# Third graph layer: elementwise work in a new order over four groups, and its own rows turned into columns by transposing transfers of SyncE

## The chip, the cores and the metric

The kernel runs on one core of one Trainium2 chip. A core has a matrix engine (TensorE, PE), a vector engine (VectorE, DVE), a scalar engine (ScalarE, ACT), a general engine (GpSimd, POOL), a queueing engine (SyncE, SP), and 16 DMA engines that move data between HBM and on-chip memory (SBUF) and inside SBUF. The matrix engine writes into PSUM, here eight banks of 128 partitions x 512 fp32. Each engine runs its own instruction stream in order, and streams meet only at semaphores. The metric is the device time of one execution in microseconds (us).

## What is computed

Four graph layers on 4096 nodes with 128 features each, every one as `x = x + layer(relu(layernorm(x)))`, over one 4096 x 4096 adjacency matrix of zeros and ones: an attention layer, a mean-aggregation layer, a gated layer (GRU), and a hyperbolic layer. The change touches the third:

```python
h = relu(layernorm(x))
agg = adj @ h
msg = relu(agg @ W_msg.T + b_msg)
gi = msg @ W_ih.T + b_ih
gh = h @ W_hh.T + b_hh                       # the layer's own rows
r = sigmoid(i_r + h_r)
z = sigmoid(i_z + h_z)
n = tanh(i_n + r * h_n)
x = x + (1 - z) * n + z * h
```

and the first half of the fourth, which the kernel computes group by group beside it:

```python
h = relu(layernorm(x))
e = exp_map_zero(log_map_zero(h) @ embed)    # norms, artanh, tanh per row
e = h_add(e, embed_bias)                     # a point in the ball
t = log_map_zero(e)                          # its tangent: operand of adj @ t
p1 = h @ layer[:128]                         # stored, used later
```

`adj @ t` and everything behind it is the fourth layer's second half and is not changed.

## The kernel before

**Tiling.** The 4096 rows are 32 tiles of 128 rows, and 8 groups of 4 tiles (`NT`, `TG`, `NG`). Most 128 x 512 operations handle one group. The adjacency matrix stays in SBUF as fp8. An operand row is held as two fp16 parts, a high and a low one, so a product with the adjacency matrix takes 64 matmuls of 128 x 512 for a group of output columns (32 tiles times 2 parts): one *step*. Steps are numbered through: 8 to 15 (`s`) are the third layer's aggregations, 16 to 23 the fourth's; 16 to 19 are called FIRST to FOURTH. A step's matmuls are `k` = 0 to 63 (L1432).

**TensorE's order** is written by hand. The tables `after`, `late`, `back` and `own` (L1381 to L1386) say at which `k` of a step a small piece of another group is put in. Take group `g`, whose aggregation is step `g+8`. During the step after it, TensorE does `hidden_gates` (k = 1: nine matmuls of L1286, own rows as columns `hT16` times three weight matrices, into banks 4, 5, 7), `message` (k = 6), `message_gates` (k = 11, L1329 to L1331) and `update_back` (k = 44: transposes of L1336, which bring the new state back into rows). One step later follow `new_transposes` (k = 15), `embed` (k = 26) and `own_part` (k = 32; L1279). `own_transposes` (k = 62 of the group's own step, L1272) turns the group's rows, kept in `hs_b` (a part of `region_op`), into columns in bank 2; ScalarE copies them into `hT16` (L1061).

**ScalarE and VectorE** each run one function `layer2` per iteration, for three groups at once: group `g` (gates, update), group `g-1` (new rows, their norms, embedding) and group `g-2` (ball point, tangent). Iterations 2 to 7 are a hardware loop. Semaphore names say what is ready: `u_ready` the updated state, `row16_ready` the new rows in two parts, `z_ready` the ball point, `coef_ready` the factor of its tangent, `hs_ready` an operand group, `rz_ready` the two sigmoid gates, `t_ready` the argument of the tanh of `n`. VectorE sums `hT16`'s two parts at L790. GpSimd takes the square roots: `norm_h`, `norm_e`, `norm_z`, and `inverse_deviation`.

**SyncE** in this stretch only stores `p1_sb`, the group's own product with `layer[:128]`, into `p1_rows` in HBM (L311), one group after another; ScalarE fills the single buffer `p1_sb` at L1141 after waiting for the store of the group before (`p1_out`), and takes a tanh (L1083) right behind it.

**The end of the layer.** Behind step 15 TensorE has FIRST to FOURTH as filling, cut into pieces (L1497 to L1516): FIRST, SECOND and THIRD can run up to k = 56 and FOURTH to k = 24 before they need `hs_ready` of the last group, the end of its chain.

Of the kernel before, what the change touches and what calls it, by code (L numbers as in the profile page):

```python
# [17 lines left out]
D = 128  # L18
NT = N // P
TG = 4  # L20
# [35 lines left out]
BANKS_3 = (0, 1, 6, 7)  # L56
UNITS = ((0, 1), (2, 3), (4, 5), (6,), (7,))
# [16 lines left out]
def build_graph_stack(nc, x_rows, adj_pieces, proj, consts0, matrices, vectors, p1_rows, out_rows):  # L74
# [8 lines left out]
    with ExitStack() as ctx:  # L83
# [96 lines left out]
        def pair(i, part):  # L180
# [4 lines left out]
        STEPS_2 = 59  # L185
# [44 lines left out]
            "pre_tr", "pre_hT", "agg_full", "aThi_ready", "aT_ready", "l1_self", "l1_neigh",  # L230
# [49 lines left out]
        def _(sp):  # L280
# [59 lines left out]
        def _(dve):  # L340
# [421 lines left out]
            def layer2(a, b, c):  # L762
                A, B, E = a is not None, b is not None, c is not None
                if A:
                    low_aggregate(a, NG)
                if B:

                    dve.wait_ge(S["rs_ready"], b + 2 * NG + 1)
                    normalised(b, lambda t: tile(dT, t)).then_inc(S["xnew_ready"], 1)
                if E:  # L770
                    ball_rows(lambda t: tile(bank[3], t), b3e)
                if B:
                    dve.wait_ge(S["row16hi_ready"], b + 1)
                    v.scalar_tensor_tensor(row16[:, 1, :, :], tiles(dT), 0.0, row16[:, 0, :, :], ALU.max,
                                           ALU.subtract).then_inc(S["row16_ready"], 1)

                part = BOTH if B and E else H_ONLY if B else Z_ONLY
                count = b + 1 if B else NG + 1
                if E:
                    dve.wait_ge(S["nrmz_ready"], c + 1)  # L780
                if B:
                    dve.wait_ge(S["nrmh_ready"], b + 1)
                if B or E:
                    artanh_start(part)
                if B:
                    me.step(copy(ssh[:, group_of(b)], C(SSH)))
                if B or E:
                    artanh_series(part, count)
                if A:
                    me.step(v.tensor_tensor(dT, hT16[:, 0, :], hT16[:, 1, :], ALU.add))  # L790

                    dve.wait_ge(S["gates_full"], a + 1)
                    dve.wait_ge(S["rz_ready"], a + 1)
                    me.link(v.scalar_tensor_tensor(rT, bank[7], b_hn, rT, ALU.add, ALU.mult))
                    v.scalar_tensor_tensor(rT, rT, w_unsplit[:, M_HN:M_HN + 1], bank[6], ALU.mult,
                                           ALU.add).then_inc(S["t_ready"], 1)

                    dve.wait_ge(S["n_ready"], a + 1)
                    me.link(v.scalar_tensor_tensor(dT, dT, 1.0 / SPLIT, rT, ALU.mult, ALU.subtract))
                    me.link(v.tensor_tensor(zT, zT, dT, ALU.mult))  # L800
                    v.tensor_tensor(zT, zT, rT, ALU.add).then_inc(S["u_ready"], 1)
                if B or E:
                    artanh_finish(part, count)
                if E:
                    v.tensor_scalar(C(COEF), pair(KAP, Z_ONLY), SPLIT, None, ALU.mult).then_inc(S["coef_ready"], 1)
                if B:
                    dve.wait_ge(S["sqe_ready"], b + 1)
                    dots(lambda t: tile(bank[3], t), b3e, w_unsplit[:, M_EMB:M_EMB + 1])
                    dve.wait_ge(S["nrme_ready"], b + 1)
                    exp_argument(pair(KAP, H_ONLY))  # L810
                if A:
                    dve.wait_ge(S["uT_full"], a + 1)
                    v.tensor_tensor(x[:, group_of(a), :], x[:, group_of(a), :], tiles(bank[7]), ALU.add).then_inc(S["x3_ready"], 1)
                    dve.wait_ge(S["x3_ready"], a + 1)
                    statistics(a)
                if E:
                    dve.wait_ge(S["bhi_ready"], c + 1)
                    v.tensor_tensor(hs_a[:, group_of(c), 1, :], tiles(z_rows), hs_a[:, group_of(c), 0, :],
                                    ALU.subtract).then_inc(S["hs_ready"], 1)
                if B:  # L820
                    sum_coefficients(pair(KAP, H_ONLY), b + 1, y2e)
                    me.link(v.tensor_scalar(C(CA), C(CA), w_unsplit[:, M_EMB:M_EMB + 1], None, ALU.mult))
                if E:
                    dve.wait_ge(S["hs_ready"], c + 2 * NG + 1)

            layer2(0, None, None)
            layer2(1, 0, None)
            with dve.Fori(2, NG) as g:
                me.loop(g - 2, STEPS_2)
                layer2(g, g - 1, g - 2)  # L830
            me.end(NG - 2)
            layer2(None, NG - 1, NG - 2)
            layer2(None, None, NG - 1)
# [103 lines left out]
        def _(pool):  # L937
# [59 lines left out]
            with pool.Fori(1, NG) as g:  # L997
                norm_h(g - 1)
                norm_e(g - 1, 0)
                inverse_deviation(g, 2 * NG)  # L1000
                norm_z(g - 1)
            norm_h(NG - 1)
            norm_e(NG - 1, 0)
# [17 lines left out]
        def _(act):  # L1021
# [81 lines left out]
            def layer2(s, b, c):  # L1103
                A, B, E = s is not None, b is not None, c is not None
                if A:
                    if not (isinstance(s, int) and s == 0):
                        act.wait_ge(S["u_ready"], s)
                    own_rows_T(s, NG)
                    high_aggregate(s, NG, False)
                if B:  # L1110
                    act.wait_ge(S["xnew_ready"], b + 2 * NG + 1)
                    a.activation(row16[:, 0, :, :], tiles(dT), ACT.Relu).then_inc(S["row16hi_ready"], 1)
                if A:
                    act.wait_ge(S["msg_full"], s + 1)
                    a.activation(msgT, bank[6], ACT.Relu, bias=b_msg, scale=w_unscale[:, M_MSG:M_MSG + 1]).then_inc(S["msg_ready"], 1)
                if E:
                    act.wait_ge(S["z_ready"], c + 1)
                    square_sums(lambda t: tile(z_rows, t), col4(SSZ)).then_inc(S["sqz_ready"], 1)
                if B:
                    act.wait_ge(S["row16_ready"], b + 1)  # L1120
                    a.activation(dT, dT, ACT.Relu).then_inc(S["relu_ready"], 1)
                    act.wait_ge(S["relu_ready"], b + 1)
                    square_sums(lambda t: tile(dT, t), col4(SSH), 1.0 / SPLIT).then_inc(S["ssh_ready"], 1)
                if A:
                    act.wait_ge(S["gates_full"], s + 1)
                    a.activation(rT, bank[4], ACT.Sigmoid, bias=brz[:, 0:1], scale=w_unsplit[:, M_HR:M_HR + 1])
                    a.activation(zT, bank[5], ACT.Sigmoid, bias=brz[:, 1:2], scale=w_unsplit[:, M_HZ:M_HZ + 1]).then_inc(S["rz_ready"], 1)
                if B:
                    act.wait_ge(S["h3_tr"], b + 1)
                    a.activation(h3T16, tr16, ACT.Copy).then_inc(S["h3T_ready"], 1)  # L1130
                if A:
                    act.wait_ge(S["t_ready"], s + 1)
                    a.activation(rT, rT, ACT.Tanh, bias=b_ih[:, 2:3]).then_inc(S["n_ready"], 1)
                if B or E:
                    logarithms(BOTH if B and E else H_ONLY if B else Z_ONLY, b + 1 if B else NG + 1)
                if B:
                    act.wait_ge(S["emb_full"], b + 1)
                    square_sums(lambda t: tile(bank[3], t), col4(SSE), w_unsplit[:, M_EMB:M_EMB + 1]).then_inc(S["sqe_ready"], 1)
                    act.wait_ge(S["top_full"], b + 1)
                    act.wait_ge(S["p1_out"], b * 16 + 16)  # L1140
                    a.activation(p1_sb, bank[4], ACT.Copy, scale=w_unsplit[:, M_TOP:M_TOP + 1]).then_inc(S["p1_ready"], 1)  # L1141
                    tanh_of(b + 1)
                if E:
                    act.wait_ge(S["coef_ready"], c + 1)
                    act.wait_ge(S["sqz_ready"], c + 1)
                    for t in range(TG):
# [9 lines left out]
            with act.Fori(2, NG) as g:  # L1156
                layer2(g, g - 1, g - 2)
# [400 lines left out]
```

## Time and profile before

| what | us |
|---|---|
| median of 3 runs | 628.37 |
| lowest, highest | 626.72, 628.53 |
| profiled execution, its own time | 626.34 |
| its span, first to last instruction | 624.5 |
| TensorE busy | 571.3 |
| VectorE busy | 338.7 |
| ScalarE busy | 217.7 |
| GpSimd busy | 99.8 |

The profile is one execution. "Busy" is time with an instruction in work. A matmul of 128 x 512 is shown with 379 ns, from issue to end, but the next one starts before it ends, so lengths in TensorE's stream are best read from one row's start to the next one's. Times within the trace count from the span's start. The third layer's aggregation runs from 294 to 472 us, the end of its elementwise work to 527 us.

### The profile page before, as it was taken

What the parts mean: (1) busy time and instruction counts of PE and PEld (TensorE: products, weight loads), DVE (VectorE), ACT (ScalarE), POOL (GpSimd) and SP (SyncE); (2) the same over time, 40 slices, a digit from 0 to 9 for tenths busy, and PEclk for the clock granted to TensorE, in tenths of its full rate; (3) what the DMA queues carried; (4) which work ended last, traced back from release to release, by engine and by line L of the source; (5) the groups of instructions that cost most, each with busy time, mean ns of one, the idle gap of its engine ahead of it and who ended that gap; (6) DMA issues with size and microseconds to landing.
All of it is one profiled execution on the core that took longest, in us unless ns stands there. A gap on an engine that the chain in (4) does not pass through costs nothing.

```text
span 624.5 us, 12573 instructions
## 1 busy us (share of the span) xinstructions
PE 571.3 (91%) x4599; PEld 354.9 (57%) x4599; DVE 338.7 (54%) x1483; ACT 217.7 (35%) x588; POOL 99.8 (16%) x104
## 2 busy tenths in 40 slices
PE   5589999999899899999999998998999899999981
PEld 5489899999754455554444453443544444554541
DVE  5872553221333433333434866866866844577786
ACT  5430000000001111111125586686686573523433
POOL 4860100000000000000001121111111110321311
PEclk9879999999999999999999999999999999999996
DMA  8999999999900000000000000000000011101000
GB/s 230 108 108 108 108 109 109 108 108 109 96 2 2 1 1 1 0 1 1 1 0 1 18 18 2 17 18 1 17 9 10 17 38 48 34 35 52 17 35 34
DMA packets 13650, 27.01 MB, mean 43 GB/s; under 512 B 1056, under 2 KB 1696, under 8 KB 13600
## 3 DMA queue, kind: packets, MB, share of 16 engines
q0 software_dynamic: 8704, 16.78, 26.7%
q1 hardware_dynamic: 4896, 9.51, 4.4%
q8 instruction: 37, 0.61, 0.4%
q14 instruction: 13, 0.11, 0.0%
HBM read 72.43 MB, written 4.19 MB: 123 GB/s over the span
## 4 chain that ended last, share of the span: by engine, by line
PE 60%; DVE 17%; ACT 12%; issue 6%; POOL 2%; DVEq 1%; DMA 1%; another core or an unknown queue 1%; SPq 0%; ACTq 0%; POOLq 0%
PE acc L1432 35%; PE acc L1252 9%; PE acc L1253 9%; ACT w L1072 4%; PE acc L1279 3%; POOL region_st L941 2%; ACT region_st L1148 1%; DVE region_st L754 1%; ACT L1078 1%; DVE region_st L751 1%; ACT L1083 1%; DVE region_st L369 1%; PE acc L1286 1%; PE acc L1272 1%; POOL rs L941 1%
## 5 line engine op out<-in xcount | busy, mean ns | idle before, releaser
L1432 PE MATMUL acc<-adj,hs_a 128*128 128x512 fp8e4 x1024 | 230.2, 379 | 2.0 <-DVE hs_a L526 1.0
L1432 PEld LDWEIGHTS acc<-adj,hs_a 128*128 128x128 f16 x1024 | 98.6, 98 | 112.8 <-issue 1.7
L1252 PE MATMUL acc<-region_op,adj 128*128 128x133 f16 x1024 | 127.1, 224 | 8.5 <-issue 3.6
L1253 PE MATMUL acc<-region_op,adj 128*128 128x132 f16 x1024 | 127.1, 223 | 0.0
L1432 PE MATMUL acc<-adj,region_op 128*128 128x512 fp8e4 x512 | 119.6, 379 | 0.0
L1252 PEld LDWEIGHTS acc<-region_op,adj 128*128 128x128 fp8e4 x1024 | 101.1, 99 | 11.1 <-DMA adj<-adj_pieces 4.4
L1253 PEld LDWEIGHTS acc<-region_op,adj 128*128 128x128 fp8e4 x1024 | 101.1, 99 | 0.1
L1432 PEld LDWEIGHTS acc<-adj,region_op 128*128 128x128 f16 x512 | 49.0, 98 | 54.8 <-issue 4.0
L941 POOL TENSOR_TENSOR region_st<-region_st,small 128x4 f32<-128x4 f32 (+1 forms) x39 | 45.1, 1157 | 212.7 <-ACT w L1072 140.0
L941 POOL TENSOR_TENSOR rs<-rs,small 128x4 f32 (+3 forms) x27 | 30.4, 1129 | 286.5 <-DVE rs L363 268.4
L1054 ACT ACTIVATE hs_a<-rowbuf 128x512 f32 x8 | 5.0, 629 | 137.9 <-DVE rowbuf L369 137.9
L669 DVE SCALAR_TENSOR_TENSOR region_st<-acc,region_st 128x512 f16<-128x512 f16 (+1 forms) x16 | 11.1, 691 | 53.8 <-ACT region_st L1068 49.7
L497 DVE TENSOR_SCALAR deg<-acc 128x4 f32 (+1 forms) x8 | 1.3, 161 | 60.3 <-PE acc L1253 60.3
L1061 ACT ACTIVATE hT<-acc 128x1024 f16<-128x1024 f16 x16 | 16.4, 1022 | 43.1 <-PE acc L1272 43.1
L1054 ACT ACTIVATE region_op<-region_st 128x512 f32 x8 | 5.0, 629 | 67.0 <-DVE region_st L369 67.0
L1279 PE MATMUL acc<-region_st 128*128 128x128 f16 x288 | 20.0, 219 | 7.3 <-ACT region_st L1130 7.2
L1279 PEld LDWEIGHTS acc<-region_st 128*128 128x128 f16 x288 | 17.0, 98 | 15.7 <-ACT region_st L1130 10.3
L946 POOL DMA_DIRECT2D adj<-adj_pieces x32 | 23.3, 754 | 8.4 <-DMA x<-x_rows 8.4
L369 DVE TENSOR_SCALAR region_st<-x,mean,rs 128x128 f32 (+1 forms) x64 | 17.8, 341 | 10.1 <-POOL rs L941 9.8
L1072 ACT ACTIVATE w<-region_st 128x128 uint8<-128x128 f32 x64 | 19.0, 297 | 11.9 <-DVE region_st L754 11.7
L356 DVE BATCH_NORM_STATS2 small<-x 128x6 f32 (+1 forms) x96 | 20.8, 279 | 1.0
L1286 PE MATMUL acc<-hT,region_st 128*128 128x512 f16 x72 | 16.9, 380 | 3.9 <-ACT hT L1061 3.9
(238 smaller groups left out, 691.7 us busy)
## 6 DMA issues: line engine op xcount, KB each, us to landing
adj<-adj_pieces POOLq DMA_DIRECT2D x32, 512.0 KB, 66.1
p_rows<-rowbuf SPq DMA_DIRECT2D x8, 256.0 KB, 2.0
region_op<-p_rows SPq DMA_DIRECT2D x8, 256.0 KB, 3.1
out_rows<-x SPq DMA_DIRECT2D x7, 256.0 KB, 2.0
x<-x_rows SPq DMA_DIRECT2D x3, 512.0 KB, 6.7
region_st<-matrices SPq DMA_DIRECT2D x1, 768.0 KB, 8.9
x<-x_rows SPq DMA_DIRECT2D x2, 256.0 KB, 3.9
out_rows<-x SPq DMA_DIRECT2D x2, 128.0 KB, 1.7
```

The costliest lines, as they stand in the source:

```text
L356: me.step(v.bn_stats(st[:, t, :], x[:, tile_of(g, t), :].rearrange("p a d -> p (a d)")))
L369: last = v.tensor_scalar(dst(t), x[:, tile_of(g, t), :].rearrange("p a d -> p (a d)"), mean[:, tile_of(g, t)], rs[:, tile_of(g, t)], ALU.s ...
L669: v.scalar_tensor_tensor(aT16[:, 1, :], src, 1.0 / SPLIT, aT16[:, 0, :], ALU.mult, ALU.subtract).then_inc(S["aT_ready"], 1)
L941: return q.tensor_tensor(dst, src, half, ALU.pow)
L946: pool.dma_start(dst, src).then_inc(adj_in[it], 16)
L1061: a.activation(hT16, tr16, ACT.Copy).then_inc(S["pre_hT"], 1)
L1072: last = a.activation(tile(junk8, t), src(t), ACT.Square, scale=scale, accum_out=sums[:, t:t + 1])
L1252: mm(bank[TG + it % TG][:, 0:HI], adj8[:, it, jt, :], op0[:, jt, 0:HI], start=(jt == 0), stop=False)
L1253: last = mm(bank[TG + it % TG][:, 0:LO], adj8[:, it, jt, :], op0[:, jt, HI:OPW], start=False, stop=(jt == NT - 1))
L1279: last = mm(tile(dst, t), srcT[:, part, t * D:(t + 1) * D], w16[:, other, m, :], start=(part + other == 0), stop=(part == 1))
L1286: last = mm(dst, w16[:, other, m, :], srcT[:, part, :], start=(part + other == 0), stop=(stop and other == 1))
L1432: last = mm(dst, hs[:, jt, part, :], adj8[:, c * TG:(c + 1) * TG, jt, :], start=(k == 0), stop=(k == 2 * NT - 1))
```

## The change

- SyncE issues, for each group, eight transposing transfers from `hs_b` to `hT16` (128 x 128 fp16 each: 2 parts, 4 tiles). TensorE's `own_transposes` and ScalarE's copy are gone in the third layer. For group `g` SyncE waits until TensorE has used `hT16` for the group before (`hidden_full`) and VectorE has summed it (`sum_ready`).
- SyncE's store of group `g-3`'s own product stands behind the transfers of group `g`.
- The loops of VectorE and ScalarE are written out, 11 iterations over four groups: `now` (i), `before` (i-1), `second` (i-2), `third` (i-3). Each engine has a new order.
- On TensorE `message` moves from k = 6 to 9, `hidden_gates` from 1 to 10, `own_part` from 32 to 43 and ahead of `embed`, `embed` from 26 to 48, `update_back` from 44 to 53. In FIRST the last three stand at k = 36, one behind the other.
- GpSimd's `norm_z` of the group two back moves ahead of `norm_e`.

```diff
@@ SyncE
+            def transpose_own_rows(g):
+                sp.wait_ge(S["hs_ready"], NG + g + 1)
+                if g:
+                    sp.wait_ge(S["hidden_full"], g)
+                    sp.wait_ge(S["sum_ready"], g)
+                else:
+                    sp.wait_ge(S["l1_self"], NG)
+                for part in range(2):
+                    for t in range(TG):
+                        sp.dma_start(hT16[:, part, t * D:(t + 1) * D], hs_b[:, g * TG + t, part, :],
+                                     transpose=True).then_inc(S["hidden_in"], 16)
...
-            with sp.Fori(0, NG) as g:
-                sp.wait_ge(S["p1_ready"], g + 1)
-                sp.dma_start(p1_rows[:, group_of(g), :], tiles(p1_sb)).then_inc(S["p1_out"], 16)
+            for g in range(NG):
+                transpose_own_rows(g)
+                if g > 2:
+                    store_p1(g - 3)
+            for g in range(NG - 3, NG):
+                store_p1(g)
@@ VectorE
+            def hidden_sum(g):
+
+                dve.wait_ge(S["hidden_in"], (g + 1) * OWN_IN)
+                if g:
+                    dve.wait_ge(S["ssh_ready"], g)
+                v.tensor_tensor(dT, hT16[:, 0, :], hT16[:, 1, :], ALU.add).then_inc(S["sum_ready"], 1)
...
+            for i in range(NG + 3):
+                now, before, second, third = i < NG, 0 <= i - 1 < NG, 0 <= i - 2 < NG, 0 <= i - 3 < NG
+                if second:
+                    tanh_argument(i - 2)
+                if now:
+                    low_aggregate(i, NG)
+                if third:
+                    low_tangent(i - 3)
+                if before:
+                    new_rows(i - 1)
+                if second:
+                    bias_dots(i - 2)
+                if before:
+                    low_rows(i - 1)
+                if second:
+                    ball_point(i - 2)
+                if now:
+                    new_gate(i)
+                    hidden_sum(i)
+                if 0 <= i - 1 <= NG:
+                    norms_in(i - 1)
+                if now:
+                    update(i)
+                if 0 <= i - 1 <= NG:
+                    norms_out(i - 1)
+                if now:
+                    residual(i)
@@ ScalarE
-                    own_rows_T(s, NG)
...
+            for i in range(NG + 3):
+                now, before, second, third = i < NG, 0 <= i - 1 < NG, 0 <= i - 2 < NG, 0 <= i - 3 < NG
+                if second:
+                    rows_T(i - 2)
+                if 0 <= i - 2 <= NG:
+                    n = i - 2
+                    logarithms(H_ONLY if n == 0 else Z_ONLY if n == NG else BOTH, n + 1)
+                if second:
+                    embedded_squares(i - 2)
+                if third:
+                    high_tangent(i - 3)
+                if now:
+                    high_aggregate(i, NG, False)
+                if second:
+                    own_product(i - 2)
+                    tanh_of(i - 1)
+                if now:
+                    messages(i)
+                if before:
+                    high_rows(i - 1)
+                    rows_squares(i - 1)
+                if now:
+                    gates(i)
+                if second:
+                    ball_squares(i - 2)
+                if now:
+                    candidate(i)
@@ TensorE
-            own = {1: {50: own_transposes, 60: own_self}, 2: {62: own_transposes}, 3: {}}
+            own = {1: {50: own_transposes, 60: own_self}, 2: {}, 3: {}}
...
-                     2: {1: hidden_gates, 6: message, 11: message_gates},
+                     2: {9: message, 10: hidden_gates, 11: message_gates},
...
-            late = {15: new_transposes, 26: embed, 32: own_part}
-            back = {44: update_back}
+            late = {15: new_transposes, 43: own_part, 48: embed}
+            back = {53: update_back}
...
             aggregate(FIRST, 0, 36)
+            own_part(FIRST - 2)
+            embed(FIRST - 2)
             update_back(FIRST - 1)
```

How the instructions stand now. TensorE's stream around the end of a step, before: L1432 is the aggregation, L1272 the transposes, L1286 the products with the own rows and the message, L1329 to L1331 the message's gates.

```order
L1336 MATMUL acc<-ident,region_st 128x128 x3
L1432 MATMUL acc<-adj,region_op 128x512 x18
L1272 MATMUL acc<-ident,region_op 128x128 x8
L1432 MATMUL acc<-adj,region_op 128x512 x2
L1432 MATMUL acc<-adj,region_op 128x512 [waits aT_ready]
L1286 MATMUL acc<-hT,region_st 128x512 [waits x3_ready,p1_ready,rz_ready,pre_hT]
L1286 MATMUL acc<-hT,region_st 128x512 x8
L1432 MATMUL acc<-adj,region_op 128x512 x5
L1286 MATMUL acc<-region_st 128x512 [waits t_ready,aT_ready]
L1286 MATMUL acc<-region_st 128x512 x2
L1432 MATMUL acc<-adj,region_op 128x512 x5
L1329 MATMUL acc<-region_st 128x512 [waits msg_ready]
```

The same place of TensorE's stream after the change (L1521 is the aggregation, L1374 the products, L1417 the first of the message's gates, L1424 `update_back`):

```order
L1424 MATMUL acc<-ident,region_st 128x128 x3
L1521 MATMUL acc<-adj,region_op 128x512 x11
L1521 MATMUL acc<-adj,region_op 128x512 [waits aT_ready]
L1521 MATMUL acc<-adj,region_op 128x512 x8
L1374 MATMUL acc<-region_st 128x512 [waits t_ready,aT_ready]
L1374 MATMUL acc<-region_st 128x512 x2
L1521 MATMUL acc<-adj,region_op 128x512
L1374 MATMUL acc<-hT,region_st 128x512 [waits x3_ready,p1_ready,rz_ready,hidden_in]
L1374 MATMUL acc<-hT,region_st 128x512 x8
L1521 MATMUL acc<-adj,region_op 128x512
L1417 MATMUL acc<-region_st 128x512 [waits msg_ready]
```

The transposes of the own rows are gone, the products with them stand behind the message's, and between the step's end and the first of them there are now ten aggregation matmuls instead of one.

SyncE's queue in the third layer, before, one loop:

```order
L309 UNCONDITIONAL_BRANCH
L309 ISA
L311 ISA [waits p1_ready]
L311 DMA p_rows<-rowbuf 128x512
L309 REGISTER_ALU
L309 COMPARE_AND_BRANCH
```

and after the change, from group 3 on (L317 the transposing transfers, L322 the store):

```order
L317 DMA_TRANSPOSE hT<-region_op 128x128 [waits sum_ready,hidden_full,hs_ready]
L317 DMA_TRANSPOSE hT<-region_op 128x128 x7
L322 DMA p_rows<-rowbuf 128x512 [waits p1_ready]
L317 DMA_TRANSPOSE hT<-region_op 128x128 [waits sum_ready,hidden_full,hs_ready]
L317 DMA_TRANSPOSE hT<-region_op 128x128 x7
L322 DMA p_rows<-rowbuf 128x512 [waits p1_ready]
```

Each store now stands behind eight transposing transfers in the same queue.

## Rows read from the trace of the kernel before

**Rows 1.** Page: busy time of each engine, share of the span, instructions.

```profile
PE 571.3 (91%) x4599; PEld 354.9 (57%) x4599; DVE 338.7 (54%) x1483; ACT 217.7 (35%) x588; POOL 99.8 (16%) x104
```

**Rows 2.** TensorE's waits, 300 to 510 us: total us, times, longest us.

```profile
PE acc L1279 <- ACT region_st L1130: 7.2, 7, 1.2
PE acc L1286 <- ACT hT L1061: 3.9, 8, 0.5
```

**Rows 3.** Timeline of TensorE: start us, length us, instruction, count, [idle before].

```profile
400.41 2.12 PE L1286 MATMUL acc<-hT,region_st 128*128 128x512 f16 x9 [0.47 <-ACT hT L1061]
...
404.09 1.24 PE L1432 MATMUL acc<-adj,region_op 128*128 128x512 fp8e4 x5
405.52 1.12 PE L1329 MATMUL acc<-region_st 128*128 128x512 f32 x2 [0.19 <-ACT region_st L1115]
...
409.51 2.54 PE L1432 MATMUL acc<-adj,region_op 128*128 128x512 fp8e4 x11
413.23 0.84 PE L1279 MATMUL acc<-region_st 128*128 128x128 f16 x12 [1.17 <-ACT region_st L1130]
...
418.90 4.05 PE L1432 MATMUL acc<-adj,region_op 128*128 128x512 fp8e4 x18
422.78 0.61 PE L1272 MATMUL acc<-ident,region_op 128*128 128x128 f16 x8
423.23 0.81 PE L1432 MATMUL acc<-adj,region_op 128*128 128x512 fp8e4 x3
424.51 2.12 PE L1286 MATMUL acc<-hT,region_st 128*128 128x512 f16 x9 [0.47 <-ACT hT L1061]
```

**Rows 4.** Timeline of TensorE: first and last step of the layer, and its end.

```profile
310.31 2.12 PE L1286 MATMUL acc<-hT,region_st 128*128 128x512 f16 x9 [0.53 <-ACT hT L1061]
...
472.69 2.12 PE L1286 MATMUL acc<-hT,region_st 128*128 128x512 f16 x9 [0.47 <-ACT hT L1061]
...
507.10 1.51 PE L1279 MATMUL acc<-region_st 128*128 128x128 f16 x24 [1.12 <-ACT region_st L1130]
...
527.49 7.94 PE L1432 MATMUL acc<-adj,hs_a 128*128 128x512 fp8e4 x36 [0.31 <-DVE hs_a L818]
```

**Rows 5.** Timeline of VectorE, one iteration of the loop.

```profile
423.20 0.17 DVE L733 RECIPROCAL region_st<-region_st 128x4 f32<-128x4 f32 x1
...
425.49 0.23 DVE L822 TENSOR_SCALAR region_st<-region_st 128x4 f32<-128x4 f32 x1
...
428.15 1.12 DVE L751 TENSOR_SCALAR region_st<-acc,region_st 128x128 f32<-128x128 f32 x4
...
430.36 0.69 DVE L774 SCALAR_TENSOR_TENSOR region_st<-region_st 128x512 f16<-128x512 f32 x1
434.78 0.17 DVE L695 TENSOR_SCALAR region_st<-region_st 128x8 f32<-128x8 f32 x1 [3.73 <-POOL region_st L941]
...
436.50 0.68 DVE L790 TENSOR_TENSOR region_st<-hT 128x512 f32<-128x512 f16 x1
...
437.88 0.75 DVE L795 SCALAR_TENSOR_TENSOR region_st<-region_st,acc 128x512 f32<-128x512 f32 x1
439.41 0.69 DVE L799 SCALAR_TENSOR_TENSOR region_st<-region_st 128x512 f32<-128x512 f32 x1 [0.79 <-ACT region_st L1133]
```

**Rows 6.** Timeline of ScalarE, the same iteration.

```profile
428.27 0.63 ACT L1112 ACTIVATE region_st<-region_st 128x512 f16<-128x512 f32 x1 [3.33 <-DVE region_st L369]
...
442.28 0.69 ACT L1141 ACTIVATE rowbuf<-acc,region_st 128x512 f32<-128x512 f32 x1
...
444.28 0.21 ACT L1083 ACTIVATE region_st<-region_st 128x4 f32<-128x4 f32 x1
```

**Rows 7.** Page: DMA issues, KB each, median us from issue to landing.

```profile
p_rows<-rowbuf SPq DMA_DIRECT2D x8, 256.0 KB, 2.0
...
out_rows<-x SPq DMA_DIRECT2D x2, 128.0 KB, 1.7
```

**Rows 8.** Timeline of SyncE's queue: four issues one behind the other.

```profile
2.12 1.85 SPq L283 DMA_DIRECT2D x<-x_rows  x4
```

More of the change, by code:

```diff
@@ L56 @@
 BANKS_3 = (0, 1, 6, 7)
+OWN_IN = 2 * TG * 16
 UNITS = ((0, 1), (2, 3), (4, 5), (6,), (7,))
@@ L757, in ball_rows @@
                 last.then_inc(S["z_ready"], 1)
[L762 to L804, printed above, removed]
-                    v.tensor_scalar(C(COEF), pair(KAP, Z_ONLY), SPLIT, None, ALU.mult).then_inc(S["coef_ready"], 1)
[L806 to L833, printed above, removed]
+            def event(n):
+                part = H_ONLY if n == 0 else Z_ONLY if n == NG else BOTH
+                return part, n + 1
+            def new_rows(g):
+                dve.wait_ge(S["rs_ready"], g + 2 * NG + 1)
+                normalised(g, lambda t: tile(dT, t)).then_inc(S["xnew_ready"], 1)
@@ new lines, in low_rows, with norms_in @@
+            def low_rows(g):
+                dve.wait_ge(S["row16hi_ready"], g + 1)
+                v.scalar_tensor_tensor(row16[:, 1, :, :], tiles(dT), 0.0, row16[:, 0, :, :], ALU.max,
+                                       ALU.subtract).then_inc(S["row16_ready"], 1)
+            def norms_in(n):
+                part, _ = event(n)
+                if n:
+                    dve.wait_ge(S["nrmz_ready"], n)
+                if n < NG:
+                    dve.wait_ge(S["nrmh_ready"], n + 1)
+                artanh_start(part)
+                if n < NG:
+                    me.step(copy(ssh[:, group_of(n)], C(SSH)))
+                artanh_series(*event(n))
@@ new lines, in residual, with low_tangent @@
+            def residual(g):
+                dve.wait_ge(S["uT_full"], g + 1)
+                v.tensor_tensor(x[:, group_of(g), :], x[:, group_of(g), :], tiles(bank[7]), ALU.add).then_inc(S["x3_ready"], 1)
+                dve.wait_ge(S["x3_ready"], g + 1)
+                statistics(g)
+            def low_tangent(g):
+                dve.wait_ge(S["bhi_ready"], g + 1)
+                v.tensor_tensor(hs_a[:, group_of(g), 1, :], tiles(z_rows), hs_a[:, group_of(g), 0, :],
+                                ALU.subtract).then_inc(S["hs_ready"], 1)
+                dve.wait_ge(S["hs_ready"], g + 2 * NG + 1)
@@ L1100, in _ @@
                 high_part(g, NG, tiles(dT), hs_b, ACT.Relu)
[L1103 to L1107, printed above, removed]
-                    own_rows_T(s, NG)
[L1109 to L1146, printed above, removed]
-                        r = tile(z_rows, t)
-                        last = a.activation(r, r, ACT.Copy, scale=col4(COEF)[:, t:t + 1])
-                    last.then_inc(S["zs_ready"], 1)
-                    act.wait_ge(S["zs_ready"], c + 1)
-                    a.activation(hs_a[:, group_of(c), 0, :], tiles(z_rows), ACT.Copy).then_inc(S["bhi_ready"], 1)
@@ L1308, in hidden_gates @@
             def hidden_gates(s):
[L1309 removed]
+                pe.wait_ge(S["hidden_in"], (s - NG + 1) * OWN_IN)
                 if s > NG:
@@ L1349, in own_part @@
             def own_part(s):
+                pe.wait_ge(S["h3T_ready"], s - NG + 1)
                 if s > NG:
@@ L1423, in aggregate @@
                         after[(s - 1) // NG + 1][k](s - 1)
-                    if k in late and NG <= s - 2 < 2 * NG - 1:
+                    if k in late and NG <= s - 2 < 2 * NG - 1 and (s < FIRST or k < 36):
                         late[k](s - 2)
@@ L1503, in _ @@
             new_transposes(FIRST - 1)
+            own_part(FIRST - 1)
             embed(FIRST - 1)
-            own_part(FIRST - 1)
             aggregate(FIRST, 40, 48)
```

90 lines of the change are left out of this document (78 added, 12 removed).

## The prediction

> **What bounds the kernel now.** Read the busy shares first: TensorE has work 91% of the span, no other engine more than 54% [rows 1], so elementwise work costs time only where TensorE waits for it. Next read TensorE's waits in the third layer: they are few and named, 7.2 us for ScalarE's copy of the new rows as columns (L1130) and 3.9 us for its copy of the own rows as columns (L1061) [rows 2]. Then read the timeline of one step to see what a step is made of [rows 3]. From one `hidden_gates` to the next it is 24.10 us (400.41 to 424.51). Eighteen aggregation matmuls take 3.88 us from start to start (418.90 to 422.78), so one takes 0.2156 us and the step's 64 take 13.80. A run of n such matmuls ought to be followed by the next piece after n x 0.2156; what is more is a stall, and it is longer than the idle time printed, because that counts from the modelled end of the last matmul. Five from 404.09 end at 405.17, the message's gates start at 405.52: 0.35. Eleven from 409.51 end at 411.88, `embed` starts at 413.23: 1.35. Three from 423.23 end at 423.88, `hidden_gates` starts at 424.51: 0.63. Together 2.33 us of stalls in a step [rows 3].
>
> **What TensorE loses and gains.** The own transposes take 0.45 us from start to start (422.78 to 423.23) [rows 3] and go. If all three stalls go too, a step is 24.10 - 2.33 - 0.45 = 21.32 us, of which 7.52 are small pieces. The seven steps between the first and the last `hidden_gates` take 162.38 us now (310.31 to 472.69) [rows 4]; the first of them has no pieces of an older group (0.45 for transposes, about 1.35 for the 24 matmuls of L1279, which are a row of 1.51 with its pipelined end [rows 4]). So they become 19.5 + 6 x 21.32 = 147.4, a gain of 15.0. Group 0's own transposes, ahead of them, give 0.45.
>
> **The end of the layer.** Call T the end of a step. Step 15 ends at 472.69 - 0.63 - 0.22 = 471.84, and TensorE must stop for the last group's operand until 527.49 [rows 4]: 55.65 us. Its own work in that stretch is 192 aggregation matmuls (56 of three steps, 24 of the fourth), 41.4 us, and 7.52 + 1.8 of small pieces, 50.7 in all; 4.9 are stalls. After the change two stalls are left by my positions below: `update_back` 1.8, and the wait for the last new rows as columns, which is the same short chain as now (1.12 plus the pipelined 0.17) [rows 4]. That makes 53.8, a gain of 1.85. The last group's chain of elementwise work, laid out at the same prices, ends at T + 53 to 54: it and TensorE's filling arrive together, so it hides nothing more and may cost up to 1 us.
>
> **Does the elementwise order keep up?** After T, ScalarE and VectorE each make one part of the aggregate, 0.6 to 0.7 us each like the two-part rows of L1112 and L774 [rows 5, 6], ready at T + 1.6. `message` is reached at T + 9 x 0.2156 = T + 1.94. VectorE then does the low tangent 0.7, new rows and dots (1.1 each, as the four of L751), low rows 0.7: T + 5.3. The ball point's coefficients take 2.5 (423.20 to 425.72), its rows 2.2 (428.15 to 430.36), new gate and hidden sum 2.1 (436.50 to 438.63): T + 12.3. Norms 1.7 (434.78 to 436.50) after 0.4 of waiting for GpSimd, the update three times 0.7: the new state at T + 16.6 [rows 5]. TensorE wants it at 53 x 0.2156 + 7.1 = T + 18.5. In FIRST it wants it at 36 x 0.2156 + 7.1 = T + 14.9, hence the 1.8 above. `own_part` waits for the new rows as columns, the cause of today's 1.35: ScalarE's tanh follows the gate's 1.5 us (T + 11.7), its copy of 1.0 ends near T + 13.6, and it stands at k = 43, T + 15.2. All three stalls go, with 0.3 to 1.9 us to spare. VectorE's present wait of 3.73 us ahead of the norms [rows 5] is filled, since the ball point and the gate now stand before it. The loops written out cost no time that a row shows. The copy of 1.0 us on ScalarE goes; nobody waits for it but `hidden_gates`.
>
> **What the transposing transfers cost.** No row shows one. Let c be the time that each of the eight takes in its queue. Below: four plain issues, one behind the other, take 1.85 us, 0.46 each [rows 8]. Above: each waits for the whole landing of the one before, 1.7 us for the smallest store with a row [rows 7]. I take 0.7, nearer to the low end, because those four issues stand 0.46 apart where no landing is shorter than 1.7 [rows 7, 8]: a queue does not wait for landings. Two circles limit c. (1) The transfers of the next group start at the hidden sum, T + 12.3, and `hidden_gates` wants them at T + 21.32 + 2.8: 11.8 us for eight, c up to 1.45. (2) The store behind them. ScalarE may fill `p1_sb` only when the earlier store has landed, and what is queued behind that wait on ScalarE is the tanh, the message, the high rows and the gates. The circle is: hidden sum, eight transfers, store landing 2.0 [rows 7], own product and tanh 2.2 (442.28 to 444.49) [rows 6], message 0.7, high rows 0.6 [rows 6], low rows 0.7, ball point 2.5 + 2.2, gate and sum 2.1 [rows 5], and 0.4 of semaphores: 13.4 + 8c. It stays under 21.32 while c is under 1.0. This circle, not the columns, is the tight one. At 0.7 both are hidden; if the cover is gone, each further 0.1 of c costs 0.8 us in each of the five steps that have such a store.
>
> The Trainium skill ("VectorE: DVE Perf Modes", section "The three transpose paths") gives 1309 ns for a 128 x 128 transpose by DMA and 390 ns on TensorE, which speaks against the change; no run here shows yet whether eight of them overlap. If they don't, the sum by that figure would be an estimate of 620.5 instead of 609.
>
> **Sum.** 15.0 + 0.45 + 1.85 = 17.3 off the profiled execution's 626.34: 609.0. That execution is 2.0 under the median (628.37) and 0.4 under the lowest run, so the median after should lie between 609 and 611, and a few tenths of small waits will be left: 610.5.
>
> **Rivals.**
> (A) As forecast, 607 to 613: 0.53.
> (B) The stalls move: VectorE finishes the residual's statistics only about 0.5 us after T and makes the low aggregate late, so `message` waits. At 1 us in each of eight steps that is 8 back: 618. For it: only 0.3 us to spare. Against: a late step also moves TensorE's later wishes. 0.12.
> (C) The transfers pass one at a time, each quicker than a landing, c from 1.1 to 1.4. At 1.3 the circle is 23.8, 2.5 more than 21.32; five steps make 12.5, of which some 1.5 is absorbed by slack: 620; the case spans 613 to 627. For it: they are small and share one queue. Against: plain issues overlap [rows 8]. 0.15. The page named above would put c here.
> (D) Slower: each transfer takes the whole 1.7 [rows 7]. The place is the store behind the transfers; the circle becomes 27.0, so 5 x 5.7 - 1.5 = 27, and circle (1) adds 1.8 in each of two early steps: 609 + 31 = 640. It decides from c = 1.46, where 5 x (8c - 7.9) - 1.5 reaches 17.3. 0.15.
> (E) The gain is mostly made but the last group's chain, now with iterations that lag by three groups, comes out far later than T + 54 and gives it back, or c lies at the break-even: within 0.3%: 0.05.
>
> **Numbers.** Likeliest 610.5. Range 606.5 to 628: it takes in A, B and C and leaves out D and a little on either side. What this kernel's measurement can tell from no change is about 0.3%, 1.9 us. Faster 0.80 (A, B, C), same 0.05 (E), slower 0.15 (D).
>
> **What would show it.** In the profile after: from `hidden_gates` to `hidden_gates` 21.3 us in six steps (B: 22.3, with the wait for VectorE's low aggregate ahead of `message`; C and D: 23.8 and 27, with ScalarE waiting for the store ahead of the own product, and TensorE for `msg_ready`). SyncE's queue: eight transfers issued within 4 to 6 us, landing before the store. TensorE's waits for L1130's successor gone except once near the end. The forecast is wrong if c is above 1.0, if the positions of VectorE are late by more than 0.3 us at T, or if the last operand group is ready later than 54 us after the last step's end.

## The result

The changed kernel takes 625.39 us (median of 20 runs, 623.5 to 628.23) against 627.72 us (20 runs, 625.73 to 628.57) for the kernel before. The ratio is 0.9968, with a 95% interval of 0.9956 to 0.998: 0.3% faster, 2.3 us, where I had forecast 17. The profiled execution has a span of 623.8 us at a mean granted clock of 0.981.

TensorE's waits in the third layer, from the trace of the changed kernel, 285 to 510 us (total us, times, longest us). L1374 are the products with the own rows and the message, L1367 `embed` and `own_part`, L1424 `update_back`, L1203 ScalarE's fill of `p1_sb`:

```profile
PE acc L1374 <- ACT rowbuf L1203: 12.9, 5, 3.2
PE acc L1367 <- ACT region_st L1181: 1.7, 2, 1.1
PE acc L1424 <- DVE region_st L837: 1.5, 1, 1.5
PE acc L1374 <- DMA hT<-region_op: 0.4, 1, 0.4
```

They answer [rows 2]. The 7.2 us for the new rows as columns are 1.7, at the end of the layer only, and the 3.9 us for the own rows as columns are a single 0.4. In their place stands a new wait: 12.9 us, in five steps, for ScalarE's fill of `p1_sb`. The wait of `update_back` comes once, at the end of the layer, as forecast; the kernel before has 0.6 us there.

The timeline of TensorE of the changed kernel, its `hidden_gates` of the eight groups, answers [rows 3, 4]:

```profile
312.50 2.10 PE L1374 MATMUL acc<-hT,region_st 128*128 128x512 f16 x9
...
332.43 2.12 PE L1374 MATMUL acc<-hT,region_st 128*128 128x512 f16 x9 [0.36 <-DMA hT<-region_op]
...
353.64 2.11 PE L1374 MATMUL acc<-hT,region_st 128*128 128x512 f16 x9
...
376.67 2.10 PE L1374 MATMUL acc<-hT,region_st 128*128 128x512 f16 x9 [1.66 <-ACT rowbuf L1203]
...
400.75 3.19 PE L1374 MATMUL acc<-hT,region_st 128*128 128x512 f16 x9 [2.68 <-ACT rowbuf L1203]
...
425.99 2.10 PE L1374 MATMUL acc<-hT,region_st 128*128 128x512 f16 x9 [2.18 <-ACT rowbuf L1203]
...
450.60 2.10 PE L1374 MATMUL acc<-hT,region_st 128*128 128x512 f16 x9 [3.21 <-ACT rowbuf L1203]
...
475.13 2.10 PE L1374 MATMUL acc<-hT,region_st 128*128 128x512 f16 x9 [3.12 <-ACT rowbuf L1203]
```

The second step takes 21.21 us (332.43 to 353.64), as forecast. From the third on they take 23.03, 24.08, 25.24, 24.61 and 24.53, a mean of 24.30; without the first of these five it is 24.62. All seven take 162.6 us, where the kernel before had 162.4 and the sum wanted 147.4. What is left of the gain shows at the end of the layer: TensorE comes to the last operand group at 526.7 us (86 matmuls behind 508.20), against 527.5 in the kernel before, and the two spans differ by 0.7 us.

SyncE's queue in the changed kernel says what ScalarE waits for (start us, length us from the first issue to the end of the last):

```profile
387.00 10.51 SPq L317 DMA_TRANSPOSE hT<-region_op  x8
397.56 0.58 SPq L322 DMA_DIRECT2D p_rows<-rowbuf  x1
411.14 10.98 SPq L317 DMA_TRANSPOSE hT<-region_op  x8
422.55 0.33 SPq L322 DMA_DIRECT2D p_rows<-rowbuf  x1
436.34 11.03 SPq L317 DMA_TRANSPOSE hT<-region_op  x8
447.41 0.58 SPq L322 DMA_DIRECT2D p_rows<-rowbuf  x1
460.94 10.94 SPq L317 DMA_TRANSPOSE hT<-region_op  x8
```

And all transposing transfers of line L317 together (duration of an issue in ns, minimum, median, maximum; time to landing in us):

```profile
L317 SPq DMA_TRANSPOSE hT<-region_op x64: 1095/1233/2216, 294.4 to 470.7; - x64
...
DMA to landing us min/median/max: 2.2/2.3/4.5
```

A transposing transfer keeps SyncE itself busy for 1.23 us in the median, against 0.33 us for most stores of the kernel before; with gaps it is 1.31 to 1.38 us each (an eighth of 10.51 and of 11.03). Eight are 10.5 to 11.0 us, and only then is the store issued. ScalarE in the same stretch:

```profile
444.62 0.60 ACT L1134 ACTIVATE region_st<-acc 128x512 f16<-128x512 f32 x1 [0.56 <-PE acc L1521]
449.77 0.69 ACT L1203 ACTIVATE rowbuf<-acc,region_st 128x512 f32<-128x512 f32 x1 [4.55 <-DMA p_rows<-rowbuf]
450.48 1.28 ACT L1149 ACT_TABLE_LOAD   x1
```

It has its part of the aggregate ready at 445.2 and stands 4.55 us until the store issued at 447.41 has landed. TensorE's `hidden_gates` write bank 4, which the fill of `p1_sb` reads, so they start at 450.60, right behind it. One turn of the circle can be read off these rows: the transfers start at 436.34 and the store at 447.41 (11.07 us), the fill starts at 449.77 (2.36 us later), and the next transfers at 460.94 (11.17 us later). Together that is 24.60 us.

### The profile page after: what moved, and what is told of

Same layout as the page of the kernel before. It is cut to its first block, busy times and chain, and to the rows that moved or that the text cites. A ratio compares the mean times of both kernels' runs of the same rounds, so it can differ in the third digit from the quotient of the medians.

```text
span 623.8 us, 12129 instructions
## 1 busy us (share of the span) xinstructions
PE 565.9 (91%) x4535; PEld 352.0 (56%) x4535; DVE 339.7 (54%) x1483; ACT 211.8 (34%) x580; POOL 100.2 (16%) x104
## 4 chain that ended last, share of the span: by engine, by line
PE 61%; DVE 14%; SPq 10%; issue 5%; ACT 4%; DMA 3%; POOL 1%; another core or an unknown queue 0%; DVEq 0%; ACTq 0%; POOLq 0%
PE acc L1521 36%; SPq L317 10%; PE acc L1340 9%; PE acc L1341 9%; PE acc L1367 3%; DMA p_rows<-rowbuf 2%; PE acc L1374 1%; ACT L1149 1%; DMA x<-x_rows 1%; DVE region_st L773 1%; DVE region_st L770 1%; POOL rs L1003 1%; PE acc L1453 1%; DVE region_st L820 1%; ACT rowbuf L1203 1%
## 5 line engine op out<-in xcount | busy, mean ns | idle before, releaser
L1521 PE MATMUL acc<-adj,hs_a 128*128 128x512 fp8e4 x1024 | 230.4, 380 | 3.3 <-DVE hs_a L545 2.3
L1521 PEld LDWEIGHTS acc<-adj,hs_a 128*128 128x128 f16 x1024 | 98.9, 98 | 114.5 <-issue 2.5
L1521 PE MATMUL acc<-adj,region_op 128*128 128x512 fp8e4 x512 | 118.6, 379 | 0.0
L1521 PEld LDWEIGHTS acc<-adj,region_op 128*128 128x128 f16 x512 | 49.3, 98 | 56.9 <-issue 4.3
L1374 PE MATMUL acc<-hT,region_st 128*128 128x512 f16 x72 | 17.9, 397 | 13.2 <-ACT rowbuf L1203 12.9
L1367 PEld LDWEIGHTS acc<-region_st 128*128 128x128 f16 x288 | 17.3, 98 | 8.7 <-DVE region_st L688 3.0
L1367 PE MATMUL acc<-region_st 128*128 128x128 f16 x288 | 19.8, 219 | 1.8 <-ACT region_st L1181 1.7
L1134 ACT ACTIVATE region_st<-acc 128x512 f16 (+1 forms) x16 | 9.5, 596 | 34.3 <-PE acc L1521 34.3
```

Of the source, the lines that this page charges most:

```text
L1367: last = mm(tile(dst, t), srcT[:, part, t * D:(t + 1) * D], w16[:, other, m, :], start=(part + other == 0), stop=(part == 1))
L1374: last = mm(dst, w16[:, other, m, :], srcT[:, part, :], start=(part + other == 0), stop=(stop and other == 1))
L1521: last = mm(dst, hs[:, jt, part, :], adj8[:, c * TG:(c + 1) * TG, jt, :], start=(k == 0), stop=(k == 2 * NT - 1))
```

## Experiments

The theory, P: the issue time of the transfers stands in SyncE's queue ahead of the store, and a circle goes through the store: hidden sum, eight issues, landing, own product, tanh, message, high and low rows, ball point, gate, hidden sum. I had written it as 13.4 + 8c, where c is the time of one transfer in the queue; with c = 1.36 it is 24.3. The rivals: Q, the new order of the elementwise work is itself too slow; R, transposing transfers disturb other work by running beside it. Each ratio below is to the kernel before, run beside the same set: 627.87 us for the first four experiments, 627.64 for the last three.

**The store first.** The store of group `g-3` can be issued before the transfers of group `g`, since its data has been ready since the start of that step.

```diff
             for g in range(NG):
-                transpose_own_rows(g)
                 if g > 2:
                     store_p1(g - 3)
+                transpose_own_rows(g)
```

> The changed kernel with one edit: SyncE puts the store of group g-3's own product ahead of the eight transposing transfers of group g, not behind them. The profile of the changed kernel shows the transfers issued 1.31 to 1.37 us apart (10.5 to 11.0 us for eight), ScalarE's own product waiting for the store up to 4.6 us in five steps, and TensorE's hidden_gates waiting for that own product 1.7 to 3.2 us. Theory P (the transfers' issue time stands ahead of the store, and the circle through the store sets a step at 13.4 + 8c = 24.3 us): the store is out of the circle, the steps fall from 23.6 - 24.6 to 21.3 - 21.8 us (what is left is the circle through the columns: hidden sum at T + 12.3, 10.9 of issues, 1 of landing, against a wish at T + 24.1), total 609 to 612 us. Rival Q (the new order of elementwise work is itself too slow, or the columns are just as late as the store): steps stay above 23 us, TensorE waits for the transfers instead, total 622 to 626.

Measured: 609.3 us (5 runs, 608.29 to 610.94), ratio 0.9711, 0.969 to 0.9732. TensorE's waits, 290 to 540 us:

```profile
PE acc L1424 <- DVE region_st L837: 1.2, 1, 1.2
PE acc L1367 <- ACT region_st L1181: 1.1, 1, 1.1
PE acc L1374 <- DMA hT<-region_op: 0.4, 1, 0.4
```

The wait for L1203 is gone. The first `hidden_gates`, the last, and three between, in the timeline:

```profile
312.49 2.10 PE L1374 MATMUL acc<-hT,region_st 128*128 128x512 f16 x9
...
396.05 2.12 PE L1374 MATMUL acc<-hT,region_st 128*128 128x512 f16 x9
...
417.52 2.12 PE L1374 MATMUL acc<-hT,region_st 128*128 128x512 f16 x9
...
438.73 2.10 PE L1374 MATMUL acc<-hT,region_st 128*128 128x512 f16 x9
...
459.93 2.11 PE L1374 MATMUL acc<-hT,region_st 128*128 128x512 f16 x9
```

Seven steps take 147.4 us, the last 21.20. Everything but the place of one instruction in SyncE's queue is as in the changed kernel, and it is worth 16 us. P is shown and Q falls. The transfers are as long as ever:

```profile
405.25 11.05 SPq L317 DMA_TRANSPOSE hT<-region_op  x8
416.35 0.57 SPq L322 DMA_DIRECT2D p_rows<-rowbuf  x1
```

They are issued until 416.30, and `hidden_gates` start at 417.52, in a step of 21.47 us instead of 21.20. So the circle through the columns only just fits, and in this one step it costs 0.3 us. In the queue each store still stands right behind eight transfers, but it is issued a group sooner: the one of 416.35 writes out what ScalarE filled in at 415.15, and its buffer is filled again only at 436.62.

**Only the new order.** The transposes are back on TensorE and ScalarE, in the changed kernel's order.

```diff
@@ SyncE
-                transpose_own_rows(g)
-                if g > 2:
-                    store_p1(g - 3)
+                store_p1(g)
@@ ScalarE
                 if now:
+                    if i:
+                        act.wait_ge(S["sum_ready"], i)
+                        act.wait_ge(S["hidden_full"], i)
+                    own_rows_T(i, NG)
                     high_aggregate(i, NG, False)
@@ TensorE
-            own = {1: {50: own_transposes, 60: own_self}, 2: {}, 3: {}}
+            own = {1: {50: own_transposes, 60: own_self}, 2: {62: own_transposes}, 3: {}}
```

> The changed kernel's order on all engines, but the own rows are turned into columns as in the kernel before: eight transposes of TensorE at k = 62 and ScalarE's copy of 1.0 us; SyncE only stores. One half of the change alone. Theory P: without the transfers no step waits for a store; a step is 21.3 + 0.45 = 21.8 us, perhaps 22.2 since ScalarE's copy stands before its part of the aggregate and message has only 0.3 us to spare: total 612 to 616. Rival Q (the order is at fault): still 23 us and more per step, 622 to 626.

Measured: 614.26 us (4 runs, 613.6 to 615.03), ratio 0.9786, 0.9766 to 0.9806. Two steps of its timeline, with the stretch ahead of `message` in the first:

```profile
377.90 2.10 PE L1374 MATMUL acc<-hT,region_st 128*128 128x512 f16 x9
...
396.31 2.54 PE L1521 MATMUL acc<-adj,region_op 128*128 128x512 fp8e4 x11
398.89 0.82 PE L1374 MATMUL acc<-region_st 128*128 128x512 f16 x3
...
399.76 2.10 PE L1374 MATMUL acc<-hT,region_st 128*128 128x512 f16 x9
...
421.62 2.10 PE L1374 MATMUL acc<-hT,region_st 128*128 128x512 f16 x9
```

A step is 21.86 us, and no step waits for a store. The order alone is worth some 13.6 of the 18.6 us that order and transfers bring together when the store stands first. The transfers are worth the other 5.0. Of the 0.66 us by which a step here is longer, 0.45 are the transposes, and 0.21 is a stall ahead of `message`: eleven matmuls from 396.31 end at 398.68, `message` starts at 398.89. It comes from ScalarE's copy, as the expectation allowed for, at half the size: the copy runs from 396.60 to 397.62, ScalarE's part of the aggregate behind it ends at 398.11 and VectorE's at 398.83. From the first long run of matmuls in step 8 to the last `hidden_gates` the two traces differ by 4.4 us (298.58 to 465.34 here, 297.60 to 459.93 with the store first); the rest of the 5.0 is within the spread of the runs.

**Half of the transfers.**

```diff
-                for part in range(2):
+                for part in range(1):
```

> The changed kernel with only the four transfers of the high part of the own rows; the low part's columns are left out, so the hidden gates work on a stale low part. Theory P: issue time halves to 5.3 us, the circle through the store becomes about 19 us and no longer binds: steps 21.2 to 21.4 us, total 608 to 611. Rival R (what costs is that transposing transfers run at all beside the rest, by contention for SBUF or the DMA engines): at most half of the loss goes, 617 or more, with longer elementwise rows. Rival Q: 622 to 626.

Measured: 608.53 us (4 runs, 608.0 to 610.73), ratio 0.9695, 0.9675 to 0.9715. The store still stands behind the transfers, but these are short:

```profile
428.05 5.43 SPq L317 DMA_TRANSPOSE hT<-region_op  x4
433.52 0.58 SPq L322 DMA_DIRECT2D p_rows<-rowbuf  x1
```

From the second `hidden_gates` on, all steps are 21.20 us. R gets no support: this kernel has half of the transfers and the one with the store first has all of them, and they are within 1 us of each other. This edit alone shortens both circles, through the store and through the columns; it is the store's new place that tells them apart.

**Only the transfers.** The kernel before with its own order, the own rows brought by SyncE, the store of group `g-2` behind the transfers of group `g`.

```diff
-            with sp.Fori(0, NG) as g:
-                sp.wait_ge(S["p1_ready"], g + 1)
-                sp.dma_start(p1_rows[:, group_of(g), :], tiles(p1_sb)).then_inc(S["p1_out"], 16)
+            for g in range(NG):
+                transpose_own_rows(g)
+                if g > 1:
+                    store_p1(g - 2)
...
-                    own_rows_T(s, NG)
...
-                pe.wait_ge(S["pre_hT"], s + 1)
+                pe.wait_ge(S["hidden_in"], (s - NG + 1) * OWN_IN)
```

> The kernel before with its own order on TensorE, VectorE and ScalarE, and only the other half of the change: eight transposing transfers per group on SyncE in place of TensorE's transposes and ScalarE's copy (the store of group g-2 behind the transfers of group g). Here hidden_gates stands at k = 1, so the columns are wanted at T + 0.2, and they can start only at the hidden sum, T + 13.6 now, perhaps 1 earlier without the copy. Theory P: 12.6 to 13.6 + 10.9 of issues + 1.1 of landing = 24.6 to 25.6 us per step against 24.1: TensorE waits for the transfers in each of seven steps, total 630 to 638, slower than before. If the transfers cost nothing in this place, removing 0.45 + 0.63 per step would give 619 to 621.

Measured: 625.11 us (10 runs, 624.0 to 626.54), ratio 0.996, 0.9948 to 0.9973. I had said 630 to 638 and slower; it is 0.4% faster. TensorE's waits:

```profile
PE acc L1307 <- DMA hT<-region_op: 9.6, 6, 2.7
PE acc L1300 <- ACT region_st L1151: 5.1, 6, 1.2
```

The mechanism is as expected: TensorE waits for the transfers in six steps. My size for it was too large. One step of the timeline:

```profile
399.22 2.12 PE L1307 MATMUL acc<-hT,region_st 128*128 128x512 f16 x9 [1.47 <-DMA hT<-region_op]
...
423.98 2.12 PE L1307 MATMUL acc<-hT,region_st 128*128 128x512 f16 x9 [2.03 <-DMA hT<-region_op]
```

The transfers between them start at 411.52, 12.3 us after `hidden_gates`, take 11.3 and land 1.1 later: 24.8. Other groups are shorter. From 351.53 to 471.58 it is 24.0 us a step, and the two steps ahead take 19.5 and 21.9, since their transfers had time. I had carried the circle's longest reading into all seven. Taken alone, the new order is worth 13.6 us and the transfers 2.8; in the changed kernel both together are worth 2.3, since the store's place in the queue takes back the rest.

**The tail filled.** On top of the store first, TensorE's filling at the end of the layer in other pieces.

```diff
-            update_back(FIRST - 1)
-            aggregate(SECOND, 0, 40)
+            aggregate(SECOND, 0, 7)
+            update_back(FIRST - 1)
+            aggregate(SECOND, 7, 40)
...
             new_transposes(FIRST - 1)
+            aggregate(THIRD, 26, 32)
             own_part(FIRST - 1)
...
-            aggregate(FOURTH, 8, 24)
+            aggregate(FOURTH, 8, 32)
```

> The kernel with the store ahead of the transfers, and its tail rearranged on TensorE only: seven matmuls of SECOND ahead of the last update_back, six of THIRD between the last new_transposes and own_part, and FOURTH run up to k = 32 before the last operand group is needed. In the profile of the kernel with the store first, TensorE waits 1.2 us for the last updated state and 1.1 us for the last new rows as columns, and the last operand group lands 0.4 us before it is asked for. Expected if TensorE's stream alone bounds the tail: 1.7 to 2.1 us less, 607.0 to 607.8 (the kernel with the store first had 609.3). If the chain of the last group bounds it, the gain is the 0.4 us of spare time: 608.9, with a new wait for the operand.

Measured: 607.98 us (5 runs, 605.89 to 609.0), ratio 0.9692, 0.9673 to 0.9711. The waits of 1.2 and 1.1 us are gone, but the two kernels were measured in different sets, and the intervals of this kernel and of the one with the store first (0.969 to 0.9732) overlap. By the medians it is 1.3 us quicker, so the expected 1.7 to 2.1 is neither shown nor excluded.

**What sets the price of a transfer.** Each 128 x 128 transfer cut into two of 64 rows.

```diff
-                        sp.dma_start(hT16[:, part, t * D:(t + 1) * D], hs_b[:, g * TG + t, part, :],
-                                     transpose=True).then_inc(S["hidden_in"], 16)
+                        for half in range(2):
+                            h0 = half * (P // 2)
+                            sp.dma_start(hT16[:, part, t * D + h0:t * D + h0 + P // 2],
+                                         hs_b[h0:h0 + P // 2, g * TG + t, part, :],
+                                         transpose=True).then_inc(S["hidden_in"], 16)
```

> What sets the price of a transposing transfer: the kernel with the store first, each 128 x 128 transfer cut into two of 64 rows, so 16 per group with the same bytes. If a transfer's price is mostly per instruction (about 1.2 us of SyncE whatever its size), a group needs 20 to 21 us of issues and the circle through the columns is 12.3 + 21 + 1 = 34 us: TensorE waits some 13 us for the transfers in most steps, total 690 to 710. If it goes by size, 16 transfers take 10.9 us as before: total 609 to 611. A plain issue on the same queue takes 0.3 to 0.6 us whatever it moves, so I expect between, 0.8 us each, 13 us per group: 620 to 630.

Measured: 695.3 us (2 runs), ratio 1.1082, 1.1051 to 1.1113. The issue line:

```profile
L319 SPq DMA_TRANSPOSE hT<-region_op x128: 1088/1228/2041, 294.0 to 542.7; - x128
```

The median issue is 1.228 us for half the size, 1.233 for the whole. At these two sizes the price is one of instructions, not of bytes. I had guessed 0.8, against the pure case that I had put beside it (690 to 710), which was right. TensorE:

```profile
PE acc L1377 <- DMA hT<-region_op: 69.0, 8, 10.5
```

TensorE waits 8.7 to 10.5 us in each of the seven steps, less than the 13 I had expected, and the first `hidden_gates` wait 3.2. A part of the time comes from the clock: behind these waits the nine matmuls take 3.5 to 4.0 us instead of 2.1.

**The store in the middle.**

```diff
                 for part in range(2):
+                    if part and g > 2:
+                        store_p1(g - 3)
                     for t in range(TG):
...
                 transpose_own_rows(g)
-                if g > 2:
-                    store_p1(g - 3)
```

> The changed kernel with the store of group g-3 in the middle of the transfers of group g, behind four and ahead of four. The circle through the store is then 13.4 + 4 x 1.37 = 18.9 us, under TensorE's 21.2, and what is left is the circle through the columns, 12.3 + 10.9 + 0.5 for the store's issue + 1 of landing = 24.7 against 24.1. Theory P (queue position ahead of the store is what counts): steps 21.3 to 21.9, total 609.5 to 613. If instead the store is slow because transposing transfers are in flight around it, it lands as late as in the changed kernel: 618 or more.

Measured: 609.8 us (4 runs, 609.33 to 611.81), ratio 0.9727, 0.9703 to 0.9751. With four transposing transfers in the queue behind it and four just issued ahead, the store no longer delays anybody:

```profile
PE acc L1374 <- DMA hT<-region_op: 1.0, 3, 0.4
```

This is all that TensorE waits for ahead of `hidden_gates`. What costs in the changed kernel is the issue time ahead of the store, not the transfers' presence in the DMA engines.

## Why the prediction was right or wrong

- **The step that failed is the price c.** I took 0.7 us for a transposing transfer, by four plain issues that stand 0.46 apart [rows 8]. It is 1.31 to 1.38. My ground was that a queue does not wait for landings, which is true here too: issues 1.3 us apart, landings 2.3 us. But I compared the wrong thing. The instruction itself holds SyncE for 1.23 us, 2.7 times the plain spacing. The Trainium skill's 1309 ns ("VectorE: DVE Perf Modes", section "The three transpose paths"), which I had kept as a rival, is given for bf16. The spacing measured here for fp16 agrees with it, 1.31 us at its shortest.
- **The circle through the store was right**, and so was the threshold: I had called it the tight one, binding from c = 1.0, with 13.4 + 8c. Once it turns, a step is 24.6 us (the mean of four is 24.62). In the turn from 436.34 the store's issue and landing take 2.36 us where I had 2.0, and all that follows takes 11.17 where I had 11.4, so the 13.4 comes out at 13.5; the transfers, until the store is issued, take 11.07. It is rival C, and I had given it 0.15.
- **Rival C's size was too small.** It said 620. I had used c = 1.3 and so a circle of 23.8; it is 0.8 us longer, which is 4.1 us in five steps, of which 2.4 come from c. TensorE's own step is 21.20 and not 21.32, another 0.6. Five steps lost 1.8, 2.9, 4.0, 3.4 and 3.3 us, 15.5 in all, against 11. The 1.5 us that I let slack absorb was about right: five full turns would have lost 17.1, but the first lost only 1.8. The place of the wait was wrong. I had TensorE waiting for `msg_ready`; it waits at `hidden_gates`, which write bank 4 and so need the own product to have been read out of it (the semaphore `p1_ready`, which stands in the order of its instructions).
- **The circle through the columns** had an error that the wrong c hid. I allowed c up to 1.45 and counted no landing. With the store first, `hidden_gates` start 1.2 us after the last issue ends (416.30 to 417.52), so the limit is about (11.8 - 1.2) / 8 = 1.3, and c stands on it. Even with the store in its right place the transfers just fit.
- **The rest of the sum was right**, as the kernel with the store first shows: steps of 21.20 (forecast 21.32), seven steps in 147.4 (147.4), no wait of VectorE's low aggregate on TensorE's path (rival B did not happen), `update_back` waiting once at the end, 1.2 us or 1.35 with the pipelined end (1.8), the last new rows 1.1 (1.12). That the seven steps agree to a tenth is in part luck: the first is 19.94 (19.5) and one is 21.47, which the other five make up for. With c under 1.0 the forecast was 609 to 610.5; that kernel takes 609.3.
- **The end of the layer**: the last operand group and TensorE's filling were said to arrive together. In the kernel with the store first the last operand group's low part runs from 509.36 for 0.69 us. TensorE has 86 of its 122 matmuls from 491.87 ahead of the need for it, 18.5 us, so until 510.4: 0.4 us apart.

```profile
491.87 26.50 PE L1521 MATMUL acc<-adj,hs_a 128*128 128x512 fp8e4 x122
```

```profile
509.36 0.69 DVE L865 TENSOR_TENSOR hs_a<-region_st,hs_a 128x512 f16<-128x512 f32 x1 [2.01 <-ACT hs_a L1218]
```

- **The chances**: slower was given 0.15 and would have needed c above 1.46. The kernel stands a tenth below that, at 0.3% faster, on the edge of what can be told from no change. With c = 1.36 my own formula gives 609 + 5 x (8c - 7.9) - 1.5 = 622.4, so most of the miss is this one term. The range 606.5 to 628 holds the time, but only because it was drawn wide enough to take in rival C; the forecast itself had ruled C unlikely.

## What to carry to other kernels

Moving work from a busy engine to a queue is not free while the queue has other customers: count the issue time of every instruction that will stand ahead of each of them, and follow who waits for the last one. Here the new transfers met their own deadline, and the cost fell on an old store behind them; it vanished when the store, whose data was long ready, was put first. If an instruction has no row in the trace, a plain one of the same queue says little of its price: here it was low by a factor of 2.7. So look for an order that holds at the upper bound too.

## What the runs showed of the hardware

- A transposing transfer of 128 x 128 fp16 within SBUF holds SyncE for 1.23 us in the median (1.10 to 2.22) and lands 2.3 us after its issue in the median; one of 64 x 128 holds it as long, 1.23 us. A plain store of 256 KB held the same queue for 0.33 us in the kernel before, and for 0.32 to 0.59 us in the changed one.
- After some of its waits TensorE comes back at a lower granted clock. In the changed kernel it had waited 2.7 us before 400.75, and the nine matmuls that follow take 3.19 us instead of 2.10. In the kernel with half-sized transfers it waited 9.35 us before 446.07, and they take 4.02. The stretches around them (length, busy us and instructions of PE, PEld, DVE, ACT, POOL, the granted clock, DMA share, GB/s), first the changed kernel, then the one with half-sized transfers:

```profile
400.70:404.20 3.50, 3.45 (x11) 1.53 (x12) 0.82 (x3) 2.73 (x5) 0.00 (x0) 0.63 0.00 0
```

```profile
446.00:451.00 5.00, 4.93 (x11) 2.01 (x12) 0.00 (x0) 0.00 (x0) 0.00 (x0) 0.50 0.14 52
```

The second is the lower of the clock's two levels, 1.2 of 2.4 GHz; the first is a mixture of both. Waits of similar length do not always bring it: before 450.60 TensorE waited 3.21 us and the nine took 2.10. What tells the two apart was not tried.
